# Two weighing steps together in two units, and full-shape projections for the narrow layer, in a three-layer attention and mixture-of-experts kernel

## The reference

```python
x = x + 0.5 * ffn(layernorm(x))     # layer 0: wide attention, then experts
x = x + attn(layernorm(x))          # layer 1: narrow attention
x = x + 0.5 * ffn(layernorm(x))     # layer 2: as layer 0
```

## Time and profile before

| | |
|---|---|
| median of 3 runs | 844.42 us (844.34 to 846.73) |
| profiled execution | 846.46 us |
| its span, first to last instruction | 844.5 us |
| mean granted TensorE clock | 0.985 |
| busy, PE / DVE / ACT / POOL | 815.6 / 669.5 / 504.1 / 364.5 us |

### The profile page before, as it was taken

The page is one execution under the profiler, slowest core; times in us unless marked ns, Lnnn a source line. Parts: engine busy times, 40 slices in busy tenths (PEclk is TensorE's granted clock), DMA queues, the critical chain, the costliest instruction groups (busy, mean ns, idle before and its releaser), DMA issues.

```text
span 844.5 us, 13469 instructions
## 1 busy us (share of the span) xinstructions
PE 815.6 (97%) x4431; PEld 310.6 (37%) x4431; DVE 669.5 (79%) x1317; ACT 504.1 (60%) x1077; POOL 364.5 (43%) x762
## 2 busy tenths in 40 slices
PE   8899999999999998999999999999999999999995
PEld 4333344334333342332323232233344334355553
DVE  6889997697679758876889999989987787674266
ACT  3266664475457636755788777767764475475541
POOL 2563427714442364445532735515151734343532
PEclk9799999999999999999999999999999999999998
DMA  3454302110110011020010322303102200000000
GB/s 106 138 138 128 101 5 57 38 58 9 35 38 2 5 41 37 3 64 17 3 49 33 85 73 54 102 2 99 54 11 68 76 2 14 1 4 13 1 14 13
DMA packets 24700, 37.83 MB, mean 45 GB/s; under 512 B 6464, under 2 KB 22080, under 8 KB 23048
## 3 DMA queue, kind: packets, MB, share of 16 engines
q1 hardware_dynamic: 24053, 35.95, 15.0%
q10 hardware_dynamic: 579, 1.03, 0.3%
HBM read 27.03 MB, written 9.11 MB: 43 GB/s over the span
## 4 chain that ended last, share of the span: by engine, by line
PE 80%; DVE 14%; issue 2%; ACT 2%; POOL 2%; DMA 0%; POOLq 0%; ACTq 0%; DVEq 0%
PE ps_out L961 17%; PE ps L900 15%; PE ps L934 13%; PE ps L1035 12%; DVE maxes L1154 9%; PE ps L1020 7%; PE ps L856 3%; PE ps_out L950 2%; PE ps L1027 2%; PE ps L922 2%; PE ps L866 1%; PE ps L998 1%; ACT probs L1359 1%; PE ps L1011 1%; PE ps L986 1%
## 5 line engine op out<-in xcount | busy, mean ns | idle before, releaser
L1359 ACT ACTIVATE probs<-ps 128x512 f32<-128x512 f32 x768 | 414.3, 598 | 225.2 <-PE ps L934 203.7
L1154 DVE TENSOR_REDUCE maxes<-ps 128x1 f32<-128x512 f32 x768 | 479.8, 681 | 53.7 <-PE ps L900 51.5
L900 PE MATMUL ps<-k_aug,q_aug 72*128 72x512 bf16 (+1 forms) x768 | 247.7, 386 | 4.3 <-issue 2.5
L934 PE MATMUL ps<-q_aug,k_aug 75*128 75x512 bf16 (+1 forms) x704 | 231.6, 383 | 2.4 <-DVE maxes L1154 0.9
L961 PE MATMUL ps_out<-probs,v_aug 128*18 128x512 f32 x1408 | 185.6, 599 | 3.0 <-ACT probs L1359 2.1
L900 PEld LDWEIGHTS ps<-k_aug,q_aug 72*128 72x128 bf16 (+1 forms) x768 | 64.9, 97 | 169.2 <-issue 117.0
L1035 PE MATMUL ps<-w,hidden 128*128 128x512 f32 x256 | 118.7, 596 | 0.0
L934 PEld LDWEIGHTS ps<-q_aug,k_aug 75*128 75x128 bf16 (+1 forms) x704 | 59.0, 97 | 131.4 <-issue 83.8
L1251 DVE TENSOR_TENSOR prod<-ps,gate 128x512 f32<-128x512 f32 x56 | 38.7, 691 | 53.6 <-PE ps L1035 43.0
L1471 POOL TENSOR_SCALAR max_parts<-maxes 128x16 bf16<-128x16 f32 (+1 forms) x38 | 11.0, 290 | 141.7 <-DVE maxes L1154 141.5
L1551 POOL TENSOR_TENSOR prod<-prod 128x512 f32<-128x512 f32 x28 | 35.5, 1267 | 76.9 <-DVE prod L1251 57.4
(11 more groups left out here) (159 smaller groups left out, 770.1 us busy)
## 6 DMA issues: line engine op xcount, KB each, us to landing
q_aug<-qk_parts SPq DMA_DIRECT2D x7, 1152.0 KB
k_aug<-qk_parts SPq DMA_DIRECT2D x21, 384.0 KB
qk_parts<-parts SPq DMA_DIRECT2D x48, 128.0 KB, 2.3
q_aug<-qk_parts SPq DMA_DIRECT2D x11, 288.0 KB
k_aug<-qk_parts SPq DMA_DIRECT2D x24, 96.0 KB
qk_parts<-parts SPq DMA_DIRECT2D x24, 64.0 KB, 2.0
X<-in_x_dram SPq DMA_DIRECT2D x4, 256.0 KB, 4.3
w<-in_ffn_W_experts_dram SPq DMA_DIRECT2D x2, 512.0 KB, 4.2
```

Of the source, the lines that this page charges most:

```text
L900: pe.matmul(bank(use[i]), q_aug[p0:p1, r, at, qt * 128:(qt + 1) * 128], k_aug[p0:p1, r, at, :], start=True, stop=True).then_inc(bank_full[ ...
L934: pe.matmul(bank(use[i]), k_aug[p0:p1, r, at, kt * 128:(kt + 1) * 128], q_aug[p0:p1, r, at, :], start=True, stop=True).then_inc(bank_full[ ...
L1154: dve.tensor_reduce(maxes[:, u % 2, qt, at:at + 1], full(use[0]), AX.X, ALU.max).then_inc(bank_free[use[0][0]], 1)
L1359: act.activation(probs[:, step % P_RING, c:c + exp_run(u), :], both(use), ACT.Exp, scale=scale)\
```

## The change

1. `DOUBLE_UNITS`: in units 9 and 10, `weigh_v` is placed once for two steps and does both in a row (16 instructions). The scores for exponentials are placed in six of every eight places, the double step three places after its last exponential. `P_RING` stays 2.
2. q and k of a narrow unit: one matmul with the weights of q and k side by side, 128 rows (`xT` with all 128 columns of x, the weights' lower half cleared) by 128 columns. q lies in partitions 0 to 63 and k in 64 to 127 of one product, which ScalarE copies once and GpSimd splits once; SyncE stores both from there. x is turned with all its columns, and v projected from all rows.
3. The maxima are turned with all 128 columns of `max_parts` in every unit.
4. The tables of places of most units, the estimates in `HOLD`, `MAX_LATE` and `LATE_LOADS` have new values.

The diff, without most of the tables and with `part_of` and `both_parts`, which it adds:

```diff
+DOUBLE_UNITS = {9, 10}
+DOUBLE_PACE = 6
+DOUBLE_LATE = 3
...
-PREP_7 = {"norm_stats": [8], "norm_apply": [12], "x_transpose": [20], "qk_project": [21, 35], "qk_split": [28, 44],
-          "v_project": [28], "stack": [43, 59]}
+PREP_7 = {"norm_stats": [22], "norm_apply": [28], "x_transpose": [33], "qk_project": [39, 47], "qk_split": [40, 48],
+          "v_project": [36], "stack": [42, 61]}
...
-MAX_LATE = [39, 33, 23, 18, 16, 17, 22, 24, 24, 21, 16, 13, 13]
+MAX_LATE = [39, 33, 23, 18, 11, 18, 22, 24, 24, 17, 15, 13, 14]
...
-              (at["v_project"][0], ("v_project", u)),
-              (at["qk_project"][1], ("qk_project", u, 1)), (at["qk_split"][1], ("qk_split", u, 1))]
+              (at["v_project"][0], ("v_project", u))]
+    if is_ffn(u):
+        steps += [(at["qk_project"][1], ("qk_project", u, 1)), (at["qk_split"][1], ("qk_split", u, 1))]
...
-HOLD = {"x_transpose": 26, "qk_project": 31, "v_project": 32, "heads_transpose": 23, "out_project": 32,
-        "x1_transpose": 32, "logits": 32, "shared_out": 38, "expert": 33, "max_rows": 26, "heads_out": 27,
-        "mlp_up": 31, "replicate": 67, "max_scores": 28, "exp_scores": 22}
+HOLD = {"x_transpose": 32, "qk_project": 31, "v_project": 26, "heads_transpose": 23, "out_project": 35,
+        "x1_transpose": 26, "logits": 26, "shared_out": 38, "expert": 33, "max_rows": 23, "heads_out": 24,
+        "mlp_up": 25, "replicate": 61, "max_scores": 28, "exp_scores": 22}
...
-            put(together(i), "exp_scores", i // TILES, i % TILES // 4, i % 4)
+            at = i - i % 8 + i % 8 * DOUBLE_PACE // 8 if i // TILES in DOUBLE_UNITS else i
+            put(together(at), "exp_scores", i // TILES, i % TILES // 4, i % 4)
...
-        for s in range(TILES // 4):
+        for s in range(steps_at_once(u) - 1, TILES // 4, steps_at_once(u)):
             late = u * TILES + 4 * s + 3 + WEIGH_LATE
+            if u in DOUBLE_UNITS:
+                late = u * TILES + 4 * s - 4 + 7 * DOUBLE_PACE // 8 + DOUBLE_LATE
             put(late, "weigh_v", u, s)
...
-        max_parts = sb("max_parts", [128, TT * PARTS * HH], BF16)
+        max_parts = sb("max_parts", [128, 128], BF16)
...
-        awq = sb("awq", [C // 2, 3, C // 2])
+        awq = sb("awq", [C, 3, C // 2])
...
+        def both_parts(u):
+            return 1 if is_ffn(u) else 2
+        def part_of(u, qk, c):
+            if is_ffn(u):
+                return parts[:, qk, c, :]
+            return parts[qk * C // 2:(qk + 1) * C // 2, 0, c, :]
...
+                if qk == 0 and not is_ffn(u - 1):
+                    eng.wait_ge(parts_stored[1], PARTS * 16 * (u - 1))
-            h, m, l = (parts[0:rows, qk, c, :] for c in range(PARTS))
+            h, m, l = (parts[:, qk, c, :] for c in range(PARTS))
...
                     store_parts(sp, u, qk)
+                    if not is_ffn(u):
+                        store_parts(sp, u, 1)
...
-                        mm = pe.transpose(o[0:rows, t * 128:(t + 1) * 128], src[:, b, t, 0:rows], ident[:, :])
+                        mm = pe.transpose(o[:, t * 128:(t + 1) * 128], src[:, b, t, :], ident[:, :])
...
+                    if u == B:
+                        pe.wait_ge(awq_padded, 1)
-                    pe.matmul(bank(use[0])[0:rows, :], (wq, wk)[qk][:, :] if ffn else awq[:, qk, :], xT[0:rows, :],
+                    pe.matmul(bank(use[0]), (wq, wk)[qk][:, :] if ffn else awq[:, 0:2, :].rearrange("k a m -> k (a m)"), xT[:, :],
...
-                    n = TT * PARTS * H // max_pieces(u)
-                    pe.transpose(bank(use[0]).bitcast(BF16)[0:n, 0:128], max_parts[:, 0:n], identb[:, :])\
+                    pe.transpose(bank(use[0]).bitcast(BF16)[:, 0:128], max_parts[:, :], identb[:, :])\
...
-                    s, = args
-                    g, kt, n = s // TT, s % TT, u * 16 + s
-                    taken(pe, "exp_scores", u, s, 4 - exp_run(u))
-                    if s == 0:
+                    last, = args
+                    taken(pe, "exp_scores", u, last, 4 - exp_run(u))
+                    if last == steps_at_once(u) - 1:
                         taken(pe, "v_project", u)
+                    for s in range(last - steps_at_once(u) + 1, last + 1):
+                        n = u * 16 + s
...
+            dve.memset(awq[C // 2:C, :, :], 0.0).then_inc(awq_padded, 1)
...
-                    ins = act.activation(qf[0:rows, :], full(use[0])[0:rows, :], ACT.Copy)
+                    ins = act.activation(qf[:, :], full(use[0]), ACT.Copy)
```

More of the change, by code:

```diff
@@ L560, in macaron @@
             (wo[:, :], w["ffn_Wo"]),
-            (awq[:, 2, :], w["attn_WvT"]),
+            (awq[0:C // 2, 2, :], w["attn_WvT"]),
             (awo[:, :], w["attn_WoT"]),
@@ L572, in macaron @@
             for g in range(2):
[L573 removed]
+                late.append((awq[0:C // 2, i, g * 32:(g + 1) * 32].rearrange("p (i d) -> p i d", i=4), of[:, g, :, :]))
         large = len(late)
@@ L664, in split @@
         def split(eng, seq, own_wait, u, qk):
-            rows = H * head_dim(u)
-            rest, _, q = (x[0:rows, :] for x in rotated(u, qk))
+            rest, _, q = rotated(u, qk)
             taken(eng, "qk_project", u, qk)
@@ L679, in split @@
                 eng.wait_ge(parts_stored[qk], PARTS * 16 * (u - qk))
-            h, m, l = (parts[0:rows, qk, c, :] for c in range(PARTS))
-            n, done = parts_before(u, qk), part_done
-            eng.tensor_copy(h, q).then_inc(done, 1)
-            eng.wait_ge(done, n + 1)
+                if qk == 0 and not is_ffn(u - 1):
+                    eng.wait_ge(parts_stored[1], PARTS * 16 * (u - 1))
+            h, m, l = (parts[:, qk, c, :] for c in range(PARTS))
+            n, done, two = parts_before(u, qk), part_done, both_parts(u)
+            eng.tensor_copy(h, q).then_inc(done, two)
+            eng.wait_ge(done, n + two)
             seq(eng.tensor_tensor(rest, q, h, ALU.subtract))
             own_wait()
-            eng.tensor_copy(m, rest).then_inc(done, 1)
-            eng.wait_ge(done, n + 2)
-            eng.tensor_tensor(l, rest, m, ALU.subtract).then_inc(done, 1)
+            eng.tensor_copy(m, rest).then_inc(done, two)
+            eng.wait_ge(done, n + 2 * two)
+            eng.tensor_tensor(l, rest, m, ALU.subtract).then_inc(done, two)
         def rank(eng, seq, own_wait, ts):
@@ L865, in _ @@
                     for t in range(TT):
-                        mm = pe.matmul(o[:, t * rows:(t + 1) * rows], xT[0:rows, t * 128:(t + 1) * 128], wv_,
+                        mm = pe.matmul(o[:, t * rows:(t + 1) * rows], xT[:, t * 128:(t + 1) * 128], wv_,
                                        start=True, stop=True)
@@ L943, in _ @@
-                    if u == LAST:
-                        g, k2 = s // 2 % 4, s % 2
-                        if s % 4 == 0:
-                            pe.wait_ge(heads_done, 2 * u + s // 4)
-                        for i, c in itertools.product(range(2), range(4)):
-                            x0 = VW * (g % 2)
-                            mm = pe.matmul(ps_out[COL * c:COL * c + 2 * VW, 0:256],
-                                           v_aug[:, r, 2 * k2 + i, 4 * (g // 2) + c, x0:x0 + 2 * VW],
-                                           probs[:, n % P_RING, c, i * 256:(i + 1) * 256],
-                                           start=(s % 4 == 0 and i == 0), stop=(s % 4 == 3 and i == 1))
-                        mm.then_inc(out_done, 1)
-                        continue
@@ L1307, in _ @@
                         pe_done(act, "v_project", u - 1)
-                    ins = act.activation(xT[0:rows, :], full(use[0])[0:rows, :], ACT.Copy)
+                    ins = act.activation(xT[:, :], full(use[0]), ACT.Copy)
                     ins.then_inc(bank_free[use[0][0]], 1)
```

118 lines of the change are left out of this document (67 added, 51 removed).

## The result

The changed kernel took 839.84 us (median, runs from 838.42 to 842.05), the kernel before 845.15 in runs beside it: ratio 0.9937, 95% interval 0.9919 to 0.9956, so 5.3 us less (3.7 to 6.9). Forecast was 835.8, with 830 to 842 as the range. The shortfall is 8.6 - 5.3 = 3.3 us. One further execution of the changed kernel took 1008.41 us at a granted clock of 0.748; it counts in the median of five and is left out of the range and of the ratio. The profiled execution took 842.05 us (span 840.2, clock 0.986), 2.2 us above its median.

A forecast was written before the change was run, and what follows sets the result against it. TensorE, busy for 97% of the span, was taken to bound the kernel. Gains of 2.7 (doubles), 3.8 (narrow projection) and 2.1 (maxima) sum to 8.6 us, taking the 844.42 median to 835.8, range 830 to 842.

The forecast's parts named there:

- three signs of being wrong: TensorE waits for ScalarE in units 9 and 10; narrow stretches lengthen by retiming; a clock drop comes where none was.
- terms 2 and 3: One q and k projection in narrow units 4 to 7, 3.8 us; maxima turned in the full shape, 2.1 us.
- Terms 2, 3 and 4: Merged narrow q and k projection, 3.8 us; full-shape maxima, 2.1 us; x turned in full shape, nothing to gain.
- Term 5: Retimed lists, HOLD estimates and maxima starts across nearly all places: taken as 0, with 3 us either way.
- Term 1: Doubled weighing in units 9 and 10: 0.20 us for each of 16 pairs, 3.2 us, net 2.7 after waits.
- the 0.5 for waits: Charge in us for waits at all 16 doubles of units 9 and 10, taken off their 3.2 us.
- the lean pair: Leanest two steps found in unit 9, 6.87 us, said to leave ScalarE 0.8 us to spare between doubles.
- rival B: Waits in units 4, 5 and at doubles shrink, a clock drop goes: 830.3 us; chance (below 833) 0.16.
- Rival A: Doubles don't save the shape's price and VectorE holds narrow units: 4.5 us gain, 839.9; chance (839 to 842) 0.16.
- C: Units 9 and 10: two probability buffers starve doubles; slower from 0.7 us a double, 850.2 at 0.9; chance 0.06.
- D: No change that tells: C by half (0.45 us a double) on top of Rival A's losses, 843 to 846; chance 0.06.

## Why the prediction was right, and where it was off

The direction and the range held, and the value fell 3.3 us short. Of the prediction's three signs of being wrong, two came true: units 6 and 7 lengthened (94.4 to 96.2), and a drop of the clock came at 683 us, where none was. That the time still fell into the range is in part luck: the lists cost less than the 3 us allowed for them, and terms 2 and 3 gave 0.9 more than forecast. The runs give a path: from before to the changed code with old lists and single steps -6.8 us; with the new lists +2.5 (0.9920 to 0.9949); with doubles -1.0. The sum is -5.3.

**Terms 2, 3 and 4 (narrow projection, maxima, x) were right.** Forecast 5.9; measured 6.8 together (5.7 to 7.9 by its interval), 4.3 and 1.8 apart. The prices 0.86, 1.06 and 0.27 are in the trace. Among narrow scores a projection costs 0.30 + 1.06 - 0.22 = 1.14 of starts, as forecast.

**Term 5 (lists, taken at 0) was wrong, and within its stated 3 us only in the changed code.** Worked out in three surroundings: +4.6 in the code of before, +2.5 in the new code with single steps, +1.7 with doubles (0.9937 less 0.9917), the last within the uncertainty. "They add no instruction" was true and not enough: with single steps units 9 and 10 go from 148.5 to 151.1 us, and three waits of 2.2 us in all stand there. That is most of the 2.5. One of them is for the norm that GpSimd's addition stretches. Units 6 and 7 also grew, from 94.7 with old lists to 96.2. The values for doubling (0.3 us under the old lists, 1.0 under the new ones, 2.9 with the squares early) suggest that its worth depends on the lists; only the last is clear of the uncertainty.

**Term 1 (doubles, net 2.7) was mis-sized, and the part of it that was mis-sized is the 0.5 for waits.** The gross gain was there: 1.84 from double to follower and 0.31 on entry make 2.60 - 2.37 = 0.23 a pair, 3.7 us against the 3.2 forecast. What is left of it can be read from the length of units 9 and 10, less the cost of the falls in them:

| doubled | before or single | gain less falls, us | so lost in waits, us |
|---|---|---|---|
| squares early, 146.7 | before, 149.0 | 2.3 | 1.4 |
| changed, 150.0 - 3.4 | before, 149.0 | 2.4 | 1.3 |
| doubling alone, 151.7 - 3.4 | before, 149.0 | 0.7 | 3.0 |
| old lists, 151.5 - 3.4 | single, 148.5 | 0.4 | 3.3 |

These are differences of single profiled executions, and the stretches are cut at exponentials, so they are good to some tenths. Waits cost three to seven times what was charged. The room that the prediction worked out for them was also too wide: ScalarE's 42.01 us less 64 exponentials at 0.52 are 8.7 us of other work a unit and not 7, so 1.1 a pair, and the spare time in the lean pair is 0.6 and not 0.8. On top comes what stood there only as a cost of 1.7 beside rival B: a fall of the clock, here 6.8 us long and worth 3.4, behind a wait of 1.62. In the profiled execution of the changed kernel it takes the whole of the term; whether it does in the others isn't shown.

**The mechanism of the shortfall** is then, in the profiled execution and in order: ScalarE does all eight exponentials of a pair close together, so the squares of unit 9 come late; GpSimd's root waits for them and for a split of maxima; behind the root stands GpSimd's addition to `X`, which by the new lists now falls on VectorE's norm and stretches it by 1.0 us; TensorE, which has no slack in a wide unit, stands 1.62 us; its clock falls. Moving x1 did not help (its wait moved to a bank), moving the squares did, by 2.8 of 3.3 us. That run moves the squares, the root and the addition together, so it doesn't tell them apart: by the traces the stretched norm is the larger part of the wait. The prediction went through what is queued behind the waiting exponential and held it to be ready early or to have time; it left out what the run of exponentials itself pushes back, and what the pushed work then meets. That the wait brings the fall is argued and not shown, since the same 1.65 us stand before a fall in one kernel and before none in another. The Trainium skill (TensorE: Matmul & The Clock Gate, HAM oscillation) ties falls of the clock to idle gaps. The changed kernel (1.62 us of wait), the later x1 (2.01) and the early squares with single steps (1.38) agree with it; the full maxima alone (1.65 and no fall) and the old lists with doubles do not, since waits of 0.60 us and less stand before the falls of the latter.

**Rival A** gave 839.9 and the time is 839.84, but its mechanism is refuted: the price of the shape is saved in a double (1.84, not 1.98), and the merge gave all of its term. A value that hits for another reason proves nothing. **B** needed waits to go: units 4 and 5 gained 2.7 us, but units 6 and 7 lost 1.8. Its mechanism is partly there. The wait of 1.66 us ahead of the fall near 334 is gone from the changed kernel and from every other run with the new lists, and four of these with the new code (the single steps, the later x1 and both with early squares) have no fall in units 4 and 5 and take 115.6 us. The profiled execution of the changed kernel has one at 338.6 all the same, for 3.4 us, behind nothing longer than this:

```profile
336.52 0.39 PE L931 MATMUL ps<-k_aug,q_aug 36*128 36x512 bf16 x1 [0.46 <-ACT probs L1392]
```

**C** is refuted as shipped: in units 9 and 10 TensorE has no wait for exponentials that the trace ends on them; its 0.7 a double is not there. Its direction is right for `DOUBLE_LATE` = 2. **D** asked for 843 and more.

Open: what decides whether the clock falls behind a wait; how much the addition beside the norm costs when nothing else is moved; how often the changed kernel falls in executions that weren't profiled (its other runs are 2.2 to 3.6 us faster than the profiled one); and which of the lists makes units 6 and 7 longer.

## What to carry to other kernels

When a producer's work is bunched (eight exponentials in a row where there were four and four), ask of every engine in the chain behind it what small job now sits behind the bunch, and follow that job to the engine that has no slack; its place in the order is worth more than its duration. Then look at what stands behind the small job in its own queue, and what that will run beside: here an addition that nobody waited for took 1.0 us from a norm on another engine. When an instruction on the path has an unusual duration, look for what ran beside it before you blame the order. Allow for a fall of the clock behind waits on a busy TensorE, as a chance and not as a fixed price: waits of about 1.65 us were followed by none, by one worth 1.7 us and by one worth 3.4. And time the retimed lists apart from the code change, in the code they are for: here they cost between 1.7 and 4.6 us by what they stood beside.

## What the runs showed of the hardware

- Between 50 and 800 us the granted clock falls for 3.4 us or for about twice that (6.8 in the changed kernel, with the squares early and single steps, and near 329 us with old lists and single steps). The same sixteen weighing instructions take 1.84 us to their follower at 2.4 GHz and 3.55 at 1.2.
- It fell behind waits of 1.38, 1.62 and 2.01 us in a TensorE otherwise busy, and also behind waits of 0.2 to 0.6 us in both doubled kernels with old lists and of 0.46 us at 338.6 in the changed kernel. With 0.69 and 0.53 it did not fall, nor with 1.65 in the kernel with the full maxima alone, where the same wait of 1.65 or 1.66 was followed by a fall in the kernel before, with the merge alone and with both. A single wait's length doesn't sort these cases.
- A norm instruction of VectorE (128x128 fp32, both large operands in SBUF) took 1.35 us in the changed kernel beside GpSimd's 128x512 fp32 addition in SBUF (1.20 us together), 1.35 to 1.40 in four other kernels with the new lists, and 0.63 with the squares early, where they met for 0.48 us; the other 31 in each of these executions took 0.33 to 0.37. VectorE's maxima, which read PSUM, took 0.68 us at the median beside such work of GpSimd (182 of them in the changed kernel) and without it.
- A run of sixteen instructions in four column strips pays for the change of the array's shape once: 1.84 us for four rounds. The Trainium skill (TensorEngine Tiling (Array Packing), Tiling Modes) has a drain only where the mode changes; the trace agrees.
- Executions of one kernel can fall in two groups: the doubled kernel with old lists ran at 837.6 to 838.7 us with a mean clock of 0.988 to 0.991 and at 840.5 to 841.3 with 0.985 to 0.986, the one with the full maxima alone at 841.0 to 842.5 with 0.989 to 0.991 and at 844.4 to 846.3 with 0.983 to 0.985. How many falls each execution had is recorded only for the profiled ones.
